# Query and key rows placed inside SBUF, one group of 32 rows and one PSUM bank per head, in a float32 attention and expert block

## The chip, the cores and the metric

One Trainium2 chip, 1 core. The metric is the device time of one execution in microseconds; the number compared is the median of the runs shown.

## The reference, cut to what matters

```python
x = x + xattn(layernorm(x), ctx)      # x (4, 256, 128), ctx (4, 64, 64), 16 heads of 8
x = x + ffn(layernorm(x))             # 32 experts, 8 per token, and a shared one
# xattn, h = layernorm(x), scale = 1/sqrt(8):
att  = where(causal, q @ k.T * scale, -inf)         # q, k, v from h, 256 x 256 per head
attc = qc @ kc.T * scale                            # qc from h, kc, vc from ctx, 256 x 64
out  = (softmax(att) @ v + softmax(attc) @ vc) @ Wp + bp
```

Everything is float32. The kernel keeps that precision by splitting a value into a rounded part (`hi`) and the rest (`lo`) and adding three products.

## The kernel before

The kernel is written engine by engine with semaphores; nothing schedules it but the order of its code. It has three parts.

*Prologue.* Tokens are normalized and transposed, and `project(b)` (PE) computes keys, queries and context queries of batch b as columns of tokens, with 128 rows (16 heads of 8). ScalarE rounds them (L699), VectorE takes the rest (L918). To get rows for the score products, SP writes keys and queries to three DRAM tensors, `key_dram`, `ckey_dram` and `query_dram` (L394, L412), and reads them back in another order (`read_keys` L425, `read_queries` L431, context keys L478). The weights' columns are permuted first, so that the writes can be made in one piece per head (`grouped`, `stacked`). What comes back is 96 rows: for each of 4 heads, 3 parts (hi, lo, hi for queries; hi, hi, lo for keys) of 8 rows. `key_blocks` holds keys block-diagonally, so that one product gives the scores of 4 heads side by side; the blocks between are constants that VectorE and ScalarE copy in (`blocks_const`, `ckey_const`), with 4 more rows of -1 that subtract each query's maximum.

*Attention.* 16 steps i, 4 batches b of 4 groups g of 4 heads. Per step, `natural(i)` (PE L1295, L1296, L1312) computes scores with queries on the partitions, in banks 0 to 3; `maxima(i)` (DVE L979, L983, L988) takes row maxima in three parts, each handed over alone; `turn_max(i)` (PE L1324) turns them to rows, `shift(i)` (ACT L714) copies 4 rows beside the queries; `scores(i, c)` (PE L1338, L1343, L1347), c = 0 to 3, computes the scores again with keys on the partitions and the maximum subtracted, each in one of two banks, 4 and 5; `exps` (ACT L725) takes one bank at a time; POOL zeroes above the diagonal (L616, L620); `attend_self` (L1360, L1365) and `attend_context` (L1372) multiply with the values, 4 heads writing to 4 different groups of 32 partitions; `copy_out` (ACT L732), `turn_out` (PE L1382) and `normalize` (DVE) finish. The order on PE is scores(i, 0 and 1), turn_max(i+1), natural(i+2), scores(i, 2), turn_out(i-2), scores(i, 3), attend(i-1). Probabilities of even steps lie in `probs_even`, of odd steps in the memory of `keys`, so that exps(1) waits until all keys are in DRAM (`wrote_k`). Batches alternate between two copies of the rows. Between the steps stand small pieces for finished batches (output projection, second norm, router).

*FFN.* 34 items, each an expert pair or the shared expert with a chunk of 512 tokens, and a last output copy.

The queue of SP is strictly in order: writes and reads of batch 0, context keys, writes of batches 1 to 3, reads of batch 1, small loads, FFN weights of 6 units, reads of batches 2 and 3, other weights. POOL writes the context keys (L394, called with `pool`), makes constants and normalizes the last four token tiles (L557).

Of the kernel before, what the change touches and what calls it, by code (L numbers as in the profile page):

```python
# [5 lines left out]
F32 = mybir.dt.float32  # L19
# [20 lines left out]
WRITES = ((0, 1), (1, 2), (2, 4))  # L40
NORM_GROUPS = ((0, 2), (2, 4), (4, 8))
SHIFT_ROW = PARTS * GROUP * D
ROWS = SHIFT_ROW + GROUP
PART = GROUP * D
EXPERTS, TOP, INNER = 32, 8, 64
# [33 lines left out]
B_NAT0, B_NATC, B_NAT1, B_ST, B_OUT, B_MISC = 0, 1, 2, 4, 6, 7  # L79
# [5 lines left out]
def build(nc, x, ctx, w, out):  # L85

    with ExitStack() as stack:
# [7 lines left out]
        key_dram = nc.dram_tensor("key_dram", (GROUP, PARTS * D, GROUPS, TOKENS), F32, kind="Internal").ap()  # L95
        ckey_dram = nc.dram_tensor("ckey_dram", (GROUP, PARTS * D, GROUPS, CTX_KEYS), F32, kind="Internal").ap()
        query_dram = nc.dram_tensor("query_dram", (GROUP, PARTS * D, GROUPS, 2, TOKENS), F32, kind="Internal").ap()
# [7 lines left out]
        key_const = sb("key_const", [P, GROUP, CTX])  # L105
        minus_half = sb("minus_half", [P, TILES])
        spread = sb("spread", [P, PAIRS, P], F32R)
# [6 lines left out]
        w_ctx = sb("w_ctx", [CTX_C, 3, C])  # L114
# [4 lines left out]
        qkc_bias = sb("qkc_bias", [4, 2, C])  # L119
# [21 lines left out]
        row_max = sb("row_max", [P, 2, 4, GROUP], F32R)  # L141
        probs_even = sb("probs_even", [P, 4, CHUNK])
# [19 lines left out]
        with ExitStack() as attention:  # L162
            queries = sb("queries", [P, 2, 2, TOKENS], F32R, until=attention)
            ckeys = sb("ckeys", [P, 2, CTX_KEYS], F32R, until=attention)
            query_rows = sb("query_rows", [P, 2, GROUPS, 2, SEQ], F32R, until=attention)
            key_blocks = sb("key_blocks", [P, 2, GROUPS, GROUP, SEQ], F32R, until=attention)
            ckey_blocks = sb("ckey_blocks", [P, GROUPS, BATCH, GROUP, CTX], F32R, until=attention)
            spread_f = sb("spread_f", [P, SPREAD_UNITS, P], until=attention)
            keys = sb("keys", [P, 2, TOKENS], F32R, until=attention)


        probs = [probs_even[:, :, :],
                 keys[:, :, :].rearrange("p h (c n) -> p (h c) n", n=CHUNK).bitcast(F32)]
# [25 lines left out]
        placed_q = [sem(f"placed_q{k}") for k in range(2)]  # L199
# [188 lines left out]
        def write_keys(sp, dram, parts, rounded, split, done):  # L388

            sp.wait_ge(*rounded)  # L390
            for part, half in enumerate(KEY_PARTS):
                if half:
                    sp.wait_ge(*split)
# [1161 lines left out]
```

## Time and profile before

| | us |
|---|---|
| median of 3 runs | 251.88 |
| lowest, highest | 250.64, 252.55 |
| span of the profiled execution | 250.6 |
| the fastest run, as long as that execution | 250.64 |
| busy PE, DVE, ACT, POOL | 197.4, 159.9, 133.4, 86.1 |

The profile is of one execution on one core. PE is TensorE, PEld its weight loads (they overlap PE), DVE VectorE, ACT ScalarE, POOL GpSimd, SP the queue that issues most transfers; a small q (SPq, POOLq) means the issuing of a transfer. A row of the timeline has the start, the time from the first to the last end of the merged instructions, the engine, the line, the operation, output and inputs, the count, and in brackets the idle time of the engine before it with what ended it. Ends of matmuls are modelled and overlap, so the pace of matmuls is read from their starts. The chain of waits is followed back from the last instruction.

### The profile page before, as it was taken

How to read it: one execution, taken by the hardware profiler on the slowest of the kernel's cores; microseconds unless marked ns; L12 is line 12 of the kernel's file. 1: busy time of each engine (PE TensorE's matmuls, PEld its weight loads, DVE VectorE, ACT ScalarE, POOL GpSimd, SP SyncE). 2: the span in 40 equal slices, each digit the busy share in tenths (PEclk: the TensorE clock that was granted, in tenths of full speed). 3: DMA queues.
4: the chain of work that ended last, by engine and by line, in shares of the span. 5: the costliest groups of instructions: out<-in, count | busy, mean ns of one | idle time of the engine just before them, and what ended most of it. 6: DMA issues, size and time to landing. Idle time of an engine off the chain costs nothing.

```text
span 250.6 us, 3757 instructions
## 1 busy us (share of the span) xinstructions
PE 197.4 (79%) x1211; PEld 147.5 (59%) x1221; DVE 159.9 (64%) x349; ACT 133.4 (53%) x242; POOL 86.1 (34%) x128
## 2 busy tenths in 40 slices
PE   0789009744404999999998998887999999999984
PEld 0578007523203776777765765565788888887762
DVE  6987005850002566677788565897758888879883
ACT  5334005514301576778677787837455666565561
POOL 7684000010004454345647554234443534221000
PEclk9999999995555799999999999998999999999999
DMA  4132383222375324025010211100000310000002
GB/s 123 45 98 84 125 175 104 99 102 102 125 233 142 98 86 105 3 63 128 0 35 9 56 34 35 28 0 0 4 0 21 82 39 3 1 1 0 0 3 84
DMA packets 26053, 15.51 MB, mean 62 GB/s; under 512 B 12463, under 2 KB 24786, under 8 KB 26034
## 3 DMA queue, kind: packets, MB, share of 16 engines
q1 hardware_dynamic: 25186, 14.77, 21.1%
q0 software_dynamic: 496, 0.40, 0.7%
q8 instruction: 10, 0.16, 0.3%
q10 hardware_dynamic: 352, 0.10, 0.2%
q14 instruction: 9, 0.07, 0.1%
HBM read 9.62 MB, written 5.64 MB: 61 GB/s over the span
## 4 chain that ended last, share of the span: by engine, by line
PE 58%; DMA 11%; SPq 11%; DVE 7%; ACT 4%; issue 4%; POOL 3%; DVEq 0%; POOLq 0%; ACTq 0%
PE psum L1212 10%; PE psum L1214 9%; PE psum L1213 9%; DMA query_rows<-query_dram 6%; SPq L412 5%; DMA query_dram<-queries 5%; PE psum L1296 5%; SPq L425 3%; PE psum L1372 3%; PE psum L1360 3%; PE psum L1496 3%; PE psum L1338 3%; PE psum L1382 3%; SPq L394 2%; PE psum L1343 2%
## 5 line engine op out<-in xcount | busy, mean ns | idle before, releaser
L979 DVE TENSOR_REDUCE row_max<-psum 128x4 fp32r<-128x512 f32 x16 | 11.0, 690 | 50.2 <-PE psum L1296 50.2
L815 ACT ACTIVATE gate<-psum,bias_cols 128x512 f32<-128x512 f32 (+2 forms) x35 | 23.5, 675 | 31.2 <-PE psum L1214 31.2
L1296 PE MATMUL psum<-key_blocks,query_rows 96*128 96x512 f32 x48 | 25.0, 564 | 12.1 <-DMA query_rows<-query_dram 12.1
L1155 DVE SCALAR_TENSOR_TENSOR gated<-psum,bias_cols,gate 128x512 f32<-128x512 f32 x32 | 24.0, 749 | 10.7 <-ACT gate L815 10.0
L592 POOL TENSOR_TENSOR w_ffn_lo<-w_ffn,w_ffn_hi 128x384 fp32r<-128x384 f32 x17 | 20.4, 1200 | 25.4 <-ACT w_ffn_hi L739 25.4
L1212 PE MATMUL psum<-xT_hi,w_ffn_hi 128*128 128x512 f32 x66 | 27.2, 412 | 0.0
L1214 PE MATMUL psum<-xT_hi,w_ffn_lo 128*128 128x512 f32 x66 | 26.2, 397 | 0.0
L1213 PE MATMUL psum<-xT_lo,w_ffn_hi 128*128 128x512 f32 x66 | 25.9, 393 | 0.0
L725 ACT ACTIVATE keys<-psum 128x512 f32<-128x512 f32 x32 | 18.7, 600 | 10.0 <-DMA key_dram<-keys 7.8
L1168 DVE TENSOR_TENSOR hid<-gated,psum 128x512 f32<-128x512 f32 x32 | 21.8, 682 | 1.3 <-PE psum L1496 0.6
L725 ACT ACTIVATE probs_even<-psum 128x512 f32<-128x512 f32 x32 | 18.9, 597 | 5.5 <-PE psum L1343 4.3
L822 ACT CAST hid_hi<-hid 128x512 fp32r<-128x512 f32 (+1 forms) x33 | 20.3, 616 | 2.3 <-DVE hid L1168 1.7
L1295 PEld LDWEIGHTS psum<-causal,ident_bf 128*128 128x128 bf16 x32 | 3.2, 100 | 29.0 <-issue 28.5
L983 DVE TENSOR_REDUCE row_max<-psum 128x4 fp32r<-128x1024 f32 x16 | 19.4, 1215 | 0.6 <-PE psum L1296 0.6
L1295 PE MATMUL psum<-causal,ident_bf 128*128 128x512 bf16 x22 | 9.3, 423 | 13.0 <-DMA query_rows<-query_dram 13.0
L862 DVE TENSOR_TENSOR hid_lo<-hid,hid_hi 128x512 fp32r<-128x512 f32 (+2 forms) x27 | 18.6, 693 | 1.1 <-ACT hid_hi L822 0.9
L616 POOL TENSOR_SCALAR_AFFINE_SELECT probs_even<-probs_even 128x512 f32<-128x512 f32 x8 | 5.1, 635 | 34.0 <-ACT probs_even L725 34.0
L732 ACT COPY o_sb<-psum 128x512 f32<-128x512 f32 x16 | 9.4, 588 | 13.3 <-PE psum L1372 13.3
L1212 PE MATMUL psum<-hid_hi,w_ffn_hi 128*128 128x512 f32 (+2 forms) x35 | 14.4, 410 | 1.1 <-DVE hid_lo L862 1.0
L1343 PE MATMUL psum<-query_rows,key_blocks 100*128 100x128 f32 x64 | 10.1, 283 | 6.3 <-ACT keys L725 6.3
L1343 PEld LDWEIGHTS psum<-query_rows,key_blocks 100*128 100x128 f32 x64 | 10.3, 209 | 7.8 <-ACT keys L725 6.7
L1212 PEld LDWEIGHTS psum<-xT_hi,w_ffn_hi 128*128 128x128 f32 x66 | 12.7, 192 | 3.5 <-issue 1.0
(184 smaller groups left out, 496.1 us busy)
## 6 DMA issues: line engine op xcount, KB each, us to landing
query_rows<-query_dram SPq DMA_DIRECT2D x4, 768.0 KB, 5.8
query_dram<-queries SPq DMA_DIRECT2D x6, 256.0 KB
key_blocks<-key_dram SPq DMA_DIRECT2D x16, 96.0 KB
query_dram<-queries SPq DMA_DIRECT2D x3, 512.0 KB
w_ffn<-in_L_ffn_Wg SPq DMA_DIRECT2D x16, 64.0 KB, 2.0
w_ffn<-in_L_ffn_Wu SPq DMA_DIRECT2D x16, 64.0 KB, 2.1
w_ffn<-in_L_ffn_Wd SPq DMA_DIRECT2D x16, 64.0 KB, 2.1
key_dram<-keys SPq DMA_DIRECT2D x6, 128.0 KB
```

What stands on the lines that cost most here:

```text
L592: ins = pool.tensor_tensor(w_ffn_lo[:, k, :, :], w_ffn[:, k, :, :], w_ffn_hi[:, k, :, :].bitcast(F32), ALU.subtract).then_inc(ffn_lo, 1)
L725: act.activation(probs[i % 2][:, c, :], bank(B_ST + c % 2), ACT.Exp, scale=SCALE).then_inc(exp_done, 1)
L815: act.activation(gate[rows_of(n), n % 3, part], psum[of, B_GATE + n % 2, part], ACT.Silu, bias=bias_cols[of, BIAS_GATE + u:BIAS_GATE + u + ...
L822: act.copy(hid_hi[rows_of(n - 1), (n - 1) % 3, :], hid[rows_of(n - 1), (n - 1) % 3, :]).then_inc(hid_rounded, 1)
L983: dve.tensor_reduce(to[:, 1, :], psum[:, B_NAT1:B_NAT1 + 2, :].rearrange("p k (j c) -> p j k c", j=GROUP), AX.XY, ALU.max).then_inc(max_do ...
L1155: dve.scalar_tensor_tensor(out=gated[:, n % 3, :], in0=bank(B_UP + n % 2), scalar=bias_cols[:, BIAS_UP + u:BIAS_UP + u + 1], in1=gate[:, n ...
L1168: dve.tensor_tensor(hid[:, n % 3, :], gated[:, n % 3, :], bank(B_WIDE + n % 2), ALU.mult).then_inc(hid_done, 1)
L1212: pe.matmul(dst, w_hi, x_hi, start=start, stop=False, skip_group_check=True)
L1213: pe.matmul(dst, w_hi, x_lo, start=False, stop=False, skip_group_check=True)
L1214: return pe.matmul(dst, w_lo, x_hi, start=False, stop=stop, skip_group_check=True)
L1296: return pe.matmul(to, query_rows[0:KR, b % 2, g, 0, P * q:P * (q + 1)], blocks[:, :, P * k:P * (k + 1)], start=not diagonal, stop=True, s ...
L1343: ins = pe.matmul(psum[:, to, P * j:P * (j + 1)], key_blocks[0:ROWS, b % 2, g, j, P:SEQ], query_rows[0:ROWS, b % 2, g, 0, P:SEQ], start=Tr ...
```

## The change

Keys and queries no longer go to DRAM. The permuted weights are gone; per batch b and group g, 3 transfers copy 32 rows of `keys` to every fourth partition of `key_rows` (offset by the part), and 3 copy 32 rows of `queries` (self and context, 512 columns) to `query_rows`. The context keys are placed likewise by POOL's queue. A head then has partitions 32j to 32j + 31: 8 rows of each of 3 parts and 8 free ones (slot 3), which hold -1 in the keys and 0 in the queries. `natural(i)` first lays the mask over 4 banks and then makes 16 products, each of one head's 32 rows into that head's bank. `turn_max` passes the 4 x 128 query columns through the identity into bank 7 and adds the maxima, which are stored so that they land on the head's slot 3; `shift` copies all 128 rows to a new tile `shifted`. The scores are two rounds p of two heads, one bank per head (self scores in columns 0 to 383, context in 384 to 511), and the context scores use `ckey_pairs`, keys of two heads made by VectorE from `ckey_rows` with a mask (`parity`). One exp covers two banks. Probabilities have two copies of their own. The late token tiles are normalized by VectorE.

```diff
-        key_dram = nc.dram_tensor("key_dram", (GROUP, PARTS * D, GROUPS, TOKENS), F32, kind="Internal").ap()
...
+        def place_keys(eng, b, g):
+            mine = slice(PART * g, PART * (g + 1))
             for part, half in enumerate(KEY_PARTS):
+                eng.dma_start(key_rows[part:P:SLOT, b % 2, g, :].bitcast(F32),
+                              keys[mine, half, tokens(b)].bitcast(F32)).then_inc(placed[b % 2][g], 16)
+        def place_queries(eng, b, g):
+            mine = slice(PART * g, PART * (g + 1))
+            for part, half in enumerate(QUERY_PARTS):
+                eng.dma_start(query_rows[part:P:SLOT, b % 2, g, :, :].bitcast(F32),
+                              queries[mine, half, b, :, :].bitcast(F32)).then_inc(placed[b % 2][g], 16)
+        def place_batch(sp, b):
+            if b < 2:
+                sp.wait_ge(rows_set[b], 2)
+            sp.wait_ge(qkc_rounded, 3 * b + 1)
+            sp.wait_ge(qkc_split, 3 * b + 1)
+            for g in range(GROUPS):
+                if b >= 2:
+                    sp.wait_ge(t_max, 4 * (b - 2) + g + 1)
+                    sp.wait_ge(m_st, 8 * (b - 2) + 2 * g + 2)
+                place_keys(sp, b, g)
+                if g == 0:
+                    sp.wait_ge(qkc_rounded, 3 * b + 3)
+                    sp.wait_ge(qkc_split, 3 * b + 3)
+                place_queries(sp, b, g)
@@ sync
-            write_token_keys(sp, 0)
-            write_queries(sp, 0)
-            read_keys(sp, 0)
-            read_queries(sp, 0)
...
+            place_batch(sp, 0)
+            place_batch(sp, 1)
@@ gpsimd
+            place_ctx_keys(pool, 0)
+            pool.memset(row_max[:, :, :, :].bitcast(F32), 0.0).then_inc(max_zeroed, 1)
+            pool.memset(query_rows[:, 1, :, :, :].bitcast(F32), 0.0).then_inc(rows_set[1], 1)
+            pool.memset(key_rows[:, 1, :, :].bitcast(F32), -1.0).then_inc(rows_set[1], 1)
+            for g in range(1, GROUPS):
+                place_ctx_keys(pool, g)
@@ scalar
+                for p in parts:
+                    act.wait_ge(m_st, 2 * i + p + 1)
+                    act.activation(probs[:, i % 2, 2 * p:2 * p + 2, :], psum[:, B_ST:B_ST + 2, :], ACT.Exp,
                                    scale=SCALE).then_inc(exp_done, 1)
@@ vector
+                dve.wait_ge(m_nat, i + 1)
+                dve.tensor_reduce(at(0), heads[:, :, 0:P], AX.X, ALU.max)
+                dve.tensor_reduce(to[:, 2:4, :].rearrange("p t (j r) -> p j t r", j=GROUP)[:, :, :, SHIFT],
+                                  heads[:, :, 3 * P:4 * P].rearrange("p j (t k) -> p j t k", t=2), AX.X, ALU.max)
+                dve.tensor_reduce(at(1), heads[:, :, P:3 * P], AX.X, ALU.max).then_inc(max_done, 1)
...
             maxima(0)
-            blocks_const(3, copy=1).then_inc(key_blocks1_set, 1)
+            dve.wait_ge(have_mask, 1)
+            for g in range(GROUPS):
+                dve.wait_ge(placed_ck[g], 48)
+            for h in range(2):
+                blocks, rows, mine = ckey_pair(h)
+                dve.tensor_scalar(blocks, rows, mine, None, ALU.mult).then_inc(ckey_pairs_set, 1)
             maxima(1)
@@ tensor, natural
+                for j in range(GROUP):
+                    pe.matmul(bank(B_NAT + j).rearrange("p (h k) -> p h k", h=2)[:, :, 0:P], ident_bf[:, :],
+                              causal[:, 0:2, :], start=True, stop=False, skip_group_check=True)
+                pe.wait_ge(placed[b % 2][g], 96 * (b // 2 + 1))
+                for s, t, cols in ((0, 0, slice(0, P)), (0, 1, slice(P, 3 * P)),
+                                   (1, 0, slice(3 * P, 3 * P + CTX)), (1, 1, slice(3 * P + CTX, 4 * P))):
+                    for j in range(GROUP):
+                        mine = slice(PART * j, PART * (j + 1))
+                        against = (ckey_rows[mine, g, CTX * b:CTX * (b + 1)] if s else
+                                   key_rows[mine, b % 2, g, 0:P * (t + 1)])
+                        ins = pe.matmul(psum[:, B_NAT + j, cols], query_rows[mine, b % 2, g, s, P * t:P * (t + 1)],
+                                        against, start=False, stop=True, skip_group_check=True)
@@ tensor, scores
+                for t, cols in ((0, slice(0, SEQ)), (1, slice(SEQ, SEQ + P))):
+                    for j in (2 * p, 2 * p + 1):
+                        mine = slice(PART * j, PART * (j + 1))
+                        pe.matmul(psum[:, B_ST + j % 2, cols], key_rows[mine, b % 2, g, P * t:P * (t + 1)],
+                                  shifted[mine, i % 2, 0, P * t:SEQ], start=True, stop=True, skip_group_check=True)
```

The order of the instructions on TensorE (PE) in one step of the attention, from the first scores of step 4 on, before; `query_rows` are queries, `key_blocks` and `ckey_blocks` the block-diagonal keys:

```order
L1338 MATMUL psum<-query_rows,key_blocks 128x256 x4
L1324 MATMUL psum<-ident_r,row_max 4x128 x4
L1295 MATMUL psum<-causal,ident_bf 128x512
L1296 MATMUL psum<-key_blocks,query_rows 128x512
L1312 MATMUL psum<-ckey_blocks,query_rows 128x256 x2
L1296 MATMUL psum<-key_blocks,query_rows 128x512
L1295 MATMUL psum<-causal,ident_bf 128x512
L1296 MATMUL psum<-key_blocks,query_rows 128x512
L1343 MATMUL psum<-query_rows,key_blocks 128x128 x4
L1382 MATMUL psum<-ident,o_sb 128x128 x4
L1347 MATMUL psum<-query_rows,ckey_blocks 128x256 x2
L1360 MATMUL psum<-probs_even,value 9x256 x4
```

After, the same place; L1183 is the mask, L1194 are the products of 32 rows, L1203 the identity pass:

```order
L1222 MATMUL psum<-shifted,key_rows 128x256 x2
L1222 MATMUL psum<-shifted,key_rows 128x128 x2
L1226 MATMUL psum<-shifted,ckey_pairs 128x128 x2
L1203 MATMUL psum<-query_rows,ident_r 128x512
L1206 MATMUL psum<-ident_r,row_max 128x128 x4
L1183 MATMUL psum<-causal,ident_bf 128x2x128 x4
L1194 MATMUL psum<-key_rows,query_rows 128x128 x4
L1194 MATMUL psum<-key_rows,query_rows 128x256 x4
L1194 MATMUL psum<-ckey_rows,query_rows 128x64 x8
L1259 MATMUL psum<-ident,o_sb 128x128 x4
L1222 MATMUL psum<-shifted,key_rows 128x256 x2
L1222 MATMUL psum<-shifted,key_rows 128x128 x2
```

Three products of 512 columns and two of 256 in `natural` have become 16 of 64 to 256 columns; the scores come in two rounds instead of four, the second one behind the turned outputs.

SP's queue from the prologue's last loads on, before:

```order
L469 DMA b_wide<-in_L_xattn_bcv 128x128
L394 DMA key_dram<-keys 4x32x256 x3
L412 DMA query_dram<-queries 4x64x256 x3
L425 DMA key_blocks<-key_dram 24x4x256 x4
L431 DMA query_rows<-query_dram 96x8x256
L478 DMA ckey_blocks<-ckey_dram 24x16x64 x4
```

And after, where the second pair of rows is repeated for three further groups of batch 0 and four of batch 1 before the next load:

```order
L429 DMA w_ctx<-in_L_xattn_Wcv 64x128
L431 DMA b_wide<-in_L_xattn_bv 128x128
L431 DMA b_wide<-in_L_xattn_bcv 128x128
L359 DMA key_rows<-keys 32x256 x3
L366 DMA query_rows<-queries 32x512 x3
```

Writes and reads through DRAM have become 6 small transfers per group.

## Rows read from the trace of the kernel before

**Rows 1.** Page, busy time, share of the span and instructions of each engine

```profile
PE 197.4 (79%) x1211; PEld 147.5 (59%) x1221; DVE 159.9 (64%) x349; ACT 133.4 (53%) x242; POOL 86.1 (34%) x128
```

**Rows 2.** Busy time by stretch: bounds, length, engines (x instructions), clock, transfer share, GB/s

```profile
25.40:37.40 12.00, 0.00 (x0) 0.04 (x2) 0.38 (x1) 0.00 (x0) 0.00 (x0) 1.00 0.62 152
...
53.00:59.00 6.00, 0.34 (x2) 0.00 (x0) 1.94 (x3) 0.00 (x0) 0.00 (x0) 0.83 0.26 102
...
64.00:78.60 14.60, 1.66 (x10) 1.27 (x8) 0.00 (x0) 2.35 (x4) 0.00 (x0) 0.50 0.54 177
...
85.30:152.90 67.60, 65.68 (x605) 47.14 (x612) 47.40 (x116) 50.09 (x96) 34.46 (x60) 1.00 0.21 53
152.90:250.60 97.70, 89.50 (x405) 68.25 (x404) 76.83 (x151) 57.21 (x99) 27.70 (x24) 0.98 0.07 17
```

**Rows 3.** Chain of waits in order of time, from 12 us on: start, us, what

```profile
18.66 12.68 DMA query_dram<-queries
...
69.21 9.29 DMA query_rows<-query_dram
```

**Rows 4.** Timeline, where odd steps and step 4 begin

```profile
59.00 0.60 ACT L725 ACTIVATE keys<-psum 128x512 f32<-128x512 f32 x1 [7.85 <-DMA key_dram<-keys]
...
78.64 0.59 PE L1295 MATMUL psum<-causal,ident_bf 128*128 128x512 bf16 x1 [12.98 <-DMA query_rows<-query_dram]
...
81.19 0.95 PE L1343 MATMUL psum<-query_rows,key_blocks 100*128 100x128 f32 x4
```

**Rows 5.** Timeline of PE, first scores and one full step

```profile
45.84 0.64 PE L1338 MATMUL psum<-query_rows,key_blocks 100*128 100x256 f32 x4
...
94.75 0.73 PE L1338 MATMUL psum<-query_rows,key_blocks 100*128 100x256 f32 x4
...
95.57 0.39 PE L1295 MATMUL psum<-causal,ident_bf 128*128 128x512 bf16 x1
...
96.96 0.56 PE L1343 MATMUL psum<-query_rows,key_blocks 100*128 100x128 f32 x4
97.36 0.62 PE L1382 MATMUL psum<-ident,o_sb 128*128 128x128 f32 x4
97.74 0.48 PE L1347 MATMUL psum<-query_rows,ckey_blocks 100*128 100x256 f32 x2
98.15 0.62 PE L1360 MATMUL psum<-probs_even,value 128*9 128x256 f32 x8
98.59 0.40 PE L1365 MATMUL psum<-probs_even,value 128*9 128x128 f32 x8
98.92 0.63 PE L1372 MATMUL psum<-probs_even,cvalue 128*41 128x256 f32 x4
99.48 0.73 PE L1338 MATMUL psum<-query_rows,key_blocks 100*128 100x256 f32 x4
```

**Rows 6.** Timeline of ACT and DVE in a step, of POOL in the prologue

```profile
97.62 1.24 ACT L725 ACTIVATE keys<-psum 128x512 f32<-128x512 f32 x2 [0.45 <-PE psum L1343]
...
93.79 1.21 DVE L983 TENSOR_REDUCE row_max<-psum 128x4 fp32r<-128x1024 f32 x1
...
5.68 1.07 POOL L544 MEMSET value<- 128x1152 f32 x1
...
11.34 2.16 POOL L394 DMA_DIRECT2D ckey_dram<-ckeys  x3
...
14.14 1.45 POOL L540 TENSOR_TENSOR rstd<-var_eps,minus_half 128x4 f32<-128x4 f32 x1 [0.65 <-DVE var_eps L858]
```

**Rows 7.** Transfers: SP's issues, and the list of landings (KB each, us)

```profile
60.71 8.46 SPq L425 DMA_DIRECT2D key_blocks<-key_dram  x4
...
77.79 0.47 SPq L446 DMA_DIRECT2D w_ffn<-in_L_ffn_Wu  x1
...
88.79 3.22 SPq L425 DMA_DIRECT2D key_blocks<-key_dram  x4
...
ckey_dram<-ckeys POOLq DMA_DIRECT2D x3, 128.0 KB, 5.3
```

More of the change, by code:

```diff
@@ L367, in projected @@
                 return keys[:, half, tokens(b)]
-            return queries[:, half, n - 1, tokens(b)]
+            return queries[:, half, b, n - 1, :]
         def lo_done(n):
@@ L397, in write_token_keys @@
-        def write_token_keys(sp, n):
-            first, end = WRITES[n]
-            cols = slice(first * SEQ, end * SEQ)
-            write_keys(sp, key_dram[:, :, :, cols], keys[:, :, cols], (qkc_rounded, 3 * end - 2),
-                       (qkc_split, 3 * end - 2), wrote_k[n])
-        def write_queries(sp, n):
-            first, end = WRITES[n]
-            cols = slice(first * SEQ, end * SEQ)
-            sp.wait_ge(qkc_rounded, 3 * end)
-            for part in (0, 2, 1):
-                half = QUERY_PARTS[part]
-                if half:
-                    sp.wait_ge(qkc_split, 3 * end)
-                sp.dma_start(query_dram[:, D * part:D * (part + 1), :, :, cols].rearrange("j d g s n -> j (d g) s n"),
-                             queries[:, half, :, cols].bitcast(F32)).then_inc(wrote_q[n], 16)
@@ L531, in _ @@
             chain(pool.memset(minus_half[:, :], -0.5))
-            for name, r0 in (("bq", BIAS_Q), ("bcq", BIAS_CQ)):
-                pool.dma_start(qkc_bias[r0 - BIAS_Q:r0 - BIAS_Q + 1, 0, :], row(w[name])).then_inc(in_q_bias, 16)
+            pool.memset(key_rows[:, 0, :, :].bitcast(F32), -1.0).then_inc(rows_set[0], 1)
+            pool.memset(causal[:, :, :], 0.0).then_inc(g_chain, 1)
+            chained[0] += 1
             def first_rstd(k):
@@ L702, in _ @@
                     round_x(1)
-                    for g in range(1, 2):
-                        ins = ckey_const(g)
-                    ins.then_inc(ckey_blocks_set, 1)
                 if b == 1:
@@ L764, in _ @@
                     shift(i + 1)
-                exps(i, (1,))
                 if i == 2:
@@ L800, in _ @@
             act.wait_ge(have_ffn_bias, 1)
-            for done in wrote_q:
-                act.wait_ge(done, 48)
-            act.wait_ge(wrote_ck, 48)
+            for k in range(2):
+                for g in range(GROUPS):
+                    act.wait_ge(placed[k][g], 192)
+            for g in range(GROUPS):
+                act.wait_ge(placed_ck[g], 48)
+            act.wait_ge(m_nat, STEPS)
             for n in range(ITEMS + 1):
@@ new lines, in natural, with turn_max @@
+                ins.then_inc(m_nat, 1)
+            def turn_max(i):
+                b, g = divmod(i, GROUPS)
+                pe.wait_ge(max_done, i + 1)
+                take_misc(shift_placed, i + 1)
+                pe.matmul(bank(B_MISC).rearrange("p (s n) -> p s n", s=2), ident_r[:, :], query_rows[:, b % 2, g, :, :],
+                          start=True, stop=False, skip_group_check=True)
+                for n in range(4):
+                    ins = pe.matmul(psum[:, B_MISC, P * n:P * (n + 1)], row_max[:, i % 2, n, :],
+                                    ident_r[:, :], start=False, stop=True, skip_group_check=True)
+                ins.then_inc(t_max, 1)
```

362 lines of the change are left out of this document (107 added, 255 removed).

## The prediction

> **What bounds the kernel now.** I read the page's busy lines first: TensorE is busy 79% of the span [rows 1], which is a mean over unlike stages. The table by stretches cuts the span into them [rows 2]. From 25.4 to 37.4 no compute engine works and the transfer engines are 0.62 busy; from 53.0 to 59.0 and from 64.0 to 78.6 it is the same picture with 0.34 and 1.66 us of TensorE work. From 85.3 to 152.9, 13 of the 16 steps of the attention run, TensorE busy 65.68 of 67.6 us; from 152.9 to the end the FFN takes 97.7 us. So there are three regimes: waits on transfers ahead of 85, a stage bound by TensorE, and an FFN that the change does not edit.
>
> Third view: the chain of waits names the transfers. `query_dram<-queries` holds it for 12.68 us from 18.66 on, and 9.29 us of it ahead of step 4 are `query_rows<-query_dram` [rows 3]. ScalarE stands 7.85 us before its first exp into `keys`, since odd steps put their probabilities where the keys lie and these must have left for DRAM first; TensorE stands 12.98 us before step 4 because batch 1's rows are not there [rows 4]. Steps 0 to 2 (scores at 45.84 to scores at 85.3) so take 39.5 us, where a later step takes 67.6 / 13 = 5.2 us [rows 2, 5].
>
> Why are these transfers slow? From 53 to 59 the writes of queries keep 0.26 of the sixteen engines busy at 102 GB/s, about four engines' worth [rows 2]. The Trainium skill has a rule that fits ("DMA: Bandwidth & Descriptors", on why a DMA increments its semaphore by 16): a transfer uses the largest count up to 16 that divides the outermost dimension of both its sides. The write's outer dimension is 4 heads, the new transfers' 32 rows, so by it four engines become sixteen; the trace agrees with the four. The sum below does not use it.
>
> **The change, part by part.** (a) DRAM is out of the path. Per batch and group of heads SP now issues 3 transfers of 32 rows by 1 KB and 3 of 32 rows by 2 KB, 24 per batch. Nothing before has this shape. The low end is an issue of 0.47 us (`w_ffn`, 64 KB); the high end is `key_blocks` (96 KB, through DRAM), 3.22 / 4 = 0.81 us each when the queue was empty and 8.46 / 4 = 2.1 us behind the big writes [rows 7]. I take 0.47, since these are smaller than the 64 KB row or equal to it and have no writes ahead of them. A batch then takes 24 x 0.47 = 11.3 us. Batch 0's keys are ready about when POOL could send the context keys, 11.34 [rows 6], so it is issued by 22 and batch 1 by 34, each group landing alone; even at 0.81 a group's six take 4.9 us, less than a step. Later batches wait for a freed slot and then for 2.8 us per group: hidden by the steps, and SP's weight loads stand where they stood. The wait for `wrote_k` ahead of odd steps goes with the shared buffer.
>
> (b) What is late next at the start. TensorE projects batches 0 to 2 until 25.4 and is then ready; there `natural(0)` starts instead of at 37.4. But the first scores also need `ckey_pairs`, and their rows come over POOL's queue. Before, POOL ends its third `rstd` at 14.14 + 1.45 = 15.6; a POOL transfer costs 2.16 / 3 = 0.72 us, a memset 1.07 us per 1152 elements [rows 6]. Now behind that `rstd` stand 3 transfers (2.2), memsets of 1024 + 2048 + 1024 elements (3.8) and 9 transfers (6.5): 28.1 us. The landing takes some 2 us (a landing of 128 KB from this queue took 5.3 [rows 7]), and VectorE then makes two passes over 1024 columns, each at most the 1.21 of its reduction over as many [rows 6]. That gives 31 to 36; I take 33. VectorE stands in that wait with `maxima(1)` behind it, so step 0 also pays the maxima: 2.5 us of reductions less 1 that overlaps, +1.5. Scores at 33 and not 45.8 is 12.8 us. Steps 0 to 2 then cost 3 x 5.45 + 1.5 = 17.9 instead of 39.5: 21.6 us.
>
> (c) TensorE per step. Before, the rows add up to 99.48 - 94.75 = 4.73 us [rows 5]: the first scores and the turned maxima 0.82 (95.57 - 94.75), `natural` 1.39, the other scores 0.40 and 0.41 with the turned outputs, 0.38, between them, attention outputs 0.44 + 0.33 + 0.56. No engine waits inside it. Now `natural` has 4 mask passes of 256 columns (as many columns as before, 0.46), and 16 pieces of 32 rows, in four rounds of four heads, each head in its own rows of the array and its own bank. Do four such pieces run side by side? The nearest row is L1360: eight matmuls of 256 columns (two passes for each of four heads) in 0.44 us, where the pace of `natural` (1.39 us for 6 x 512 columns, 0.23 per 512) would make 0.93; the heads write different partitions and overlap [rows 5]. That is the same trick on the columns of the array; on its rows the trace shows nothing. Bounds: 0.10 us per round if they overlap (a 128-column piece of L1343, its weight load included, is 0.40 / 4), 0.10 us per piece if not. I take 0.12 per round: 0.46 + 0.48 + 0.12 = 1.06 us. The last 0.12 is a change of tiling: L1365 streams half of L1360's columns but takes 0.33, not 0.22, and L1372 0.56 against 0.44 for the same columns [rows 5]. The turned maxima get the identity pass of 512 columns (0.23) and weights of 128 columns instead of 4 (4 x 0.11): 0.67. The scores become twice (two rounds of tiles, two context pieces: 4 x 0.12; two changes of tiling, 0.24) = 1.44. Turned outputs 0.48, attention outputs 1.33 as before. That is 2.11 us of scores and turned maxima where 1.63 were. Sum 4.98 us, +0.25 per step, over 13 steps 3.2 us given back.
>
> A rule speaks against this part: the Trainium skill ("TensorEngine Tiling (Array Packing)", Key Properties) says that a change of tiling mode drains TensorE. The trace agrees that something is paid, 0.11 to 0.12 us beside L1365 and L1372, but the same page gives independent tiles their own loads and matmuls at once, which only the column tiles show here. By the first alone, at nine changes a step against three, the step would be near 5.3 us.
>
> (d) ScalarE and VectorE. Two exps of 512 columns take 1.24 us [rows 6]; one over two banks lies between that and 1.0, so two of them with shift and copy (one bank each, half of that row) are 3.3 to 3.7 us per step, below 4.98. The scores' two banks have no second copy: scores, exp, scores, exp in turn is 2 x (0.7 + 1.25) = 3.9 us, covered as well. VectorE reduces the same columns; 1.21 us is the largest of its three [rows 6], and they now start only when all of `natural` is done: 1.06 + 2.5 + 0.3 = 3.9 us before the banks are free, again less than a step. I cost these at nothing; if TensorE's step fell under 4 us they would set it. The copies that filled constants leave the prologue and bring nothing behind (b).
>
> Sum: -12.8 - 21.6 + 3.2 = -31.2 us. The span was 250.6, so 219.4. The profiled execution is as long as the fastest run shown (250.64), 1.3 us below the median 251.88, so I add this: **220.7 us**, 12% faster.
>
> **The rivals.** *Pieces one by one (15%).* Weight loads of the row tiles do not overlap, 0.11 us a piece: `natural` +1.28, scores +0.36, together +1.6 us a step, 26 us over 16 steps: 247. For it: L1343's pieces are paced by their loads (0.10 each for 128 columns, which at 0.23 per 512 would stream in 0.06) [rows 5]. Against it: L1360's eight overlap. The Trainium skill ("TensorE: Matmul & The Clock Gate", LDWEIGHTS) has a load cost the same for 32 rows as for 128; by that alone small pieces save nothing, which is this rival.
>
> *The start only changes its wait (7%).* POOL's chain of (b) or batch 1's transfers at 0.8 us hold the first scores to 45: 12 us lost, 233. For it: the 5.3 us landing; against it: natural(4) needs only batch 1's first group.
>
> *Slower: the clock (6%).* In the trace the granted clock is 1.00 after steady work and falls to 0.50 in the idle stretches [rows 2]. At 0.50 (1.2 GHz) `natural` takes 81.19 - 78.64 = 2.55 us instead of 1.39 [rows 4, 5]: 1.83 times. Pieces of 32 rows use a quarter of the array; if they don't keep the level up, the new step is 4.98 x 1.83 = 9.1 us, 4.1 more, 62 us over 15 steps: 282. It turns the sign where the loss passes 31 us, with more than half of the steps at 0.50.
>
> *Slower: transfers pace the steps (3%).* At 2.1 us each, 96 transfers end at 212 and the FFN only then: 10 + 202 + 12 + 97.7 = 322. The break-even is near 1.4 us per transfer, above what an empty queue shows.
>
> **How the numbers follow.** Forecast 69%, its own range 207 to 232: low with rounds at 0.10 without changes of tiling (8 x 0.02 + 0.46, so -0.6 us a step, 10 us) and scores at 29, if context keys are ready earlier than 15.6 and both passes are short (-4), high with 0.5 us more per step (8) and scores at 36 (3). Beside it 15, 7, 6 and 3%. To leave out no more than 2 in 10, the range goes to 247 and takes in pieces one by one. About 1% is what a measurement of this kernel tells from no change. Faster by over 1%: 69 + 7 + 15, 91%. The clock case is split: a partial loss that eats the gain, within 1%, 3%; the other 3 and the transfers' 3 are slower, 6%.
>
> **What would show it.** Right: `natural(0)` at 22 to 26 us, first scores at 31 to 35, no idle TensorE stretch over 3 us afterwards; starts of four L1194 pieces within 0.02 us of each other, 1.0 to 1.1 us for `natural`; the gap from step to step 5.2 to 5.6 us; FFN 97 to 98 us. Wrong: pieces 0.1 us apart, SP's small transfers at 0.8 us or more apiece, a granted clock of 0.5 in the steps, or VectorE or ScalarE named as the releaser of `natural` and scores in most steps.

## The result, and the profile after

The changed kernel took 285.58 us (median of 4 runs, 282.99 to 288.92), the kernel before 252.22 us in the same session (250.64 to 252.86): a ratio of 1.128, 95% interval 1.120 to 1.136. It is slower by 13%, where 220.7 us and 12% faster were forecast. The profiled execution is the shortest of the four, with a span of 281.2 us.

First the page of the kernel after: busy time by engine, and the TensorE clock in 40 slices of 7 us.

```profile
PE 255.7 (91%) x1477; PEld 180.3 (64%) x1477; DVE 159.7 (57%) x348; ACT 125.4 (45%) x204; POOL 87.9 (31%) x134
...
PEclk9999855555555555555555695579999999999999
```

Beside [rows 1] only TensorE changed much: 58 us more busy time. VectorE has as much as before, ScalarE less. The clock row says why: from the sixth slice to the 26th it stands, but for the 23rd and 24th, at five tenths. The stretches (bounds, length, then busy time of PE, PEld, DVE, ACT, POOL with the number of instructions, granted clock, transfer share, GB/s):

```profile
25.10:32.50 7.40, 5.25 (x61) 4.28 (x62) 5.74 (x11) 1.79 (x4) 0.53 (x2) 1.00 0.31 79
32.90:59.80 26.90, 24.04 (x161) 16.55 (x159) 10.68 (x18) 9.59 (x14) 6.57 (x13) 0.50 0.36 87
59.80:159.10 99.30, 98.78 (x633) 64.64 (x632) 36.56 (x85) 36.59 (x51) 27.68 (x49) 0.50 0.11 28
159.10:169.40 10.30, 8.69 (x87) 6.40 (x86) 5.17 (x16) 6.84 (x12) 3.31 (x6) 1.00 0.16 40
169.40:184.00 14.60, 13.96 (x83) 7.61 (x83) 4.75 (x19) 6.00 (x9) 5.08 (x8) 0.50 0.06 15
184.00:281.20 97.20, 87.93 (x396) 66.75 (x388) 75.40 (x146) 55.91 (x97) 26.32 (x23) 0.99 0.07 17
```

The stretches without TensorE work of [rows 2] are gone, as forecast. The last stretch, the FFN, takes 97.2 us, as forecast. Between them, from 59.8 us on, TensorE works almost without a gap and at half its clock: 98.78 of 99.30 us busy at 0.50 (1.2 GHz). Before, 13 steps ran with 65.68 of 67.60 us busy at 1.00 [rows 2]. The busy share is about the same in both, so it is not what separates the two levels.

The waits of the first steps don't separate them either. The kernel before had the longer ones, was also at 0.50 in this part, and rose after a short piece of full work; from 85.3 us on it stands at 1.00 [rows 2]. Its stretch ahead of that:

```profile
78.60:84.20 5.60, 5.56 (x28) 4.15 (x32) 2.41 (x5) 2.01 (x5) 4.59 (x10) 0.50 0.62 139
```

The Trainium skill ("TensorE: Matmul & The Clock Gate", Part 1) says that the throttled state is the default and that activity releases it, by how busy TensorE has been. These rows qualify it: an engine that a profile calls 99% busy can stay throttled for 99 us.

The same operations at both levels, from the timeline of TensorE in the kernel after (start, duration of the group, engine, line, tiles, rows by columns of the weights, operand, count):

```profile
62.11 0.80 PE L1194 MATMUL psum<-key_rows,query_rows 32*128 32x128 f32 x8
...
63.11 1.11 PE L1259 MATMUL psum<-ident,o_sb 128*128 128x128 f32 x4
...
160.95 0.61 PE L1183 MATMUL psum<-causal,ident_bf 128*128 128x256 bf16 x4
161.49 0.50 PE L1194 MATMUL psum<-key_rows,query_rows 32*128 32x128 f32 x8
...
162.07 0.66 PE L1259 MATMUL psum<-ident,o_sb 128*128 128x128 f32 x4
```

Sixteen pieces of `natural` with their masks take 162.07 - 160.95 = 1.12 us at 1.00. From the next rows, of one step at 0.50, masks and pieces take 63.11 - 61.11 = 2.00, and the step from one `turn_max` to the next 69.02 - 59.76 = 9.26 us:

```profile
59.76 0.79 PE L1203 MATMUL psum<-query_rows,ident_r 128*128 128x512 f32 x1
...
61.11 1.08 PE L1183 MATMUL psum<-causal,ident_bf 128*128 128x256 bf16 x4
...
69.02 0.79 PE L1203 MATMUL psum<-query_rows,ident_r 128*128 128x512 f32 x1
```

The start went as forecast. TensorE begins `natural(0)` at 25.11 and the first scores at 32.52 us (45.84 before [rows 5]):

```profile
25.11 1.06 PE L1183 MATMUL psum<-causal,ident_bf 128*128 128x256 bf16 x4
26.10 0.50 PE L1194 MATMUL psum<-key_rows,query_rows 32*128 32x128 f32 x8
...
30.78 0.50 PE L1203 MATMUL psum<-query_rows,ident_r 128*128 128x512 f32 x1 [2.15 <-DVE value L820]
...
32.52 0.43 PE L1222 MATMUL psum<-shifted,key_rows 32*128 32x256 f32 x4
```

The masks at 25.11 take 1.06 us, the pace of 0.50 (1.08 at 61.11), though the clock of the stretch reads 1.00; the pieces at 26.10 have the fast pace. So the clock row is not to be trusted everywhere: of the other executions of this kernel one reads 0.993 on average and is 3.0 us longer (284.2 us) than the profiled one, which reads 0.745. Where the two differ, the level is read here from the pace of the matmuls. SP's transfers cost 0.6 us each (three in 1.87 us) and land in 2.1 us or less; no engine waits for one after the start.

The issue of three is a row of SP's timeline; the landing, a row of the page's list of issues:

```profile
23.62 1.87 SPq L366 DMA_DIRECT2D query_rows<-queries  x3
```

```profile
query_rows<-queries SPq DMA_DIRECT2D x48, 64.0 KB, 2.1
```

### The profile page after: what moved, and what is told of

It is laid out like the page before. It is cut to its first block, busy times and chain, and to the rows that moved or that the text cites. A ratio compares the mean times of both kernels' runs of the same rounds, so it can differ in the third digit from the quotient of the medians.

```text
span 281.2 us, 4302 instructions
## 1 busy us (share of the span) xinstructions
PE 255.7 (91%) x1477; PEld 180.3 (64%) x1477; DVE 159.7 (57%) x348; ACT 125.4 (45%) x204; POOL 87.9 (31%) x134
## 4 chain that ended last, share of the span: by engine, by line
PE 76%; DVE 9%; issue 6%; POOL 4%; ACT 4%; DVEq 0%; POOLq 0%; ACTq 0%
PE psum L1110 9%; PE psum L1112 8%; PE psum L1111 8%; PE psum L1226 6%; PE psum L1222 6%; PE psum L1249 5%; PE psum L1194 5%; PE psum L1240 5%; PE psum L1183 5%; PE psum L1259 4%; PE psum L1206 4%; PE psum L1203 4%; DVE x L796 3%; POOL hid_lo L587 2%; PE psum L1243 2%
## 5 line engine op out<-in xcount | busy, mean ns | idle before, releaser
L651 ACT ACTIVATE probs<-psum 128x1024 f32<-128x1024 f32 x32 | 32.8, 1024 | 59.5 <-PE psum L1226 59.5
L565 POOL TENSOR_SCALAR_AFFINE_SELECT probs<-probs 128x512 f32<-128x512 f32 x32 | 20.4, 636 | 100.9 <-ACT probs L651 100.9
L1222 PEld LDWEIGHTS psum<-shifted,key_rows 32*128 32x128 f32 x128 | 15.1, 288 | 11.3 <-issue 10.5
L1222 PE MATMUL psum<-shifted,key_rows 32*128 32x128 f32 (+1 forms) x128 | 20.7, 417 | 1.3 <-ACT probs L651 1.2
L1226 PE MATMUL psum<-shifted,ckey_pairs 64*128 64x128 f32 x64 | 21.2, 428 | 0.0
L1226 PEld LDWEIGHTS psum<-shifted,ckey_pairs 64*128 64x128 f32 x64 | 15.3, 295 | 3.6
L1249 PE MATMUL psum<-probs,cvalue 128*41 128x256 f32 x64 | 16.9, 625 | 0.0
L1206 PEld LDWEIGHTS psum<-ident_r,row_max 128*128 128x128 f32 x64 | 16.0, 306 | 1.4
L1259 PE MATMUL psum<-ident,o_sb 128*128 128x128 f32 x64 | 15.9, 395 | 1.0 <-ACT shifted L643 0.9
L1183 PE MATMUL psum<-causal,ident_bf 128*128 128x256 bf16 x64 | 16.3, 406 | 0.0
```

What stands on the lines that cost most here:

```text
L651: act.activation(probs[:, i % 2, 2 * p:2 * p + 2, :], psum[:, B_ST:B_ST + 2, :], ACT.Exp, scale=SCALE).then_inc(exp_done, 1)
L1183: pe.matmul(bank(B_NAT + j).rearrange("p (h k) -> p h k", h=2)[:, :, 0:P], ident_bf[:, :], causal[:, 0:2, :], start=True, stop=False, skip ...
L1206: ins = pe.matmul(psum[:, B_MISC, P * n:P * (n + 1)], row_max[:, i % 2, n, :], ident_r[:, :], start=False, stop=True, skip_group_check=True)
L1222: pe.matmul(psum[:, B_ST + j % 2, cols], key_rows[mine, b % 2, g, P * t:P * (t + 1)], shifted[mine, i % 2, 0, P * t:SEQ], start=True, stop ...
L1226: ins = pe.matmul(psum[:, B_ST + t, 3 * P:4 * P], ckey_pairs[pair, g, b, :, :].rearrange("p h k -> p (h k)"), shifted[pair, i % 2, 1, P * ...
L1249: ins = pe.matmul(psum[64 * j:64 * j + 32 + D + 1, B_OUT, SEQ:2 * SEQ], cvalue[:, b, 2 * g + j, :], probs[:, i % 2, 2 * j:2 * j + 2, 3 * P ...
```

## The experiments

Thirteen more kernels ran. Theory A: TensorE stays at its low level because most products of the new step use 32 or 64 rows of the array. Theory B: the waits of the first steps, or the changes of tiling, bring it down. Theory C: columns per time count, not rows. The tool of most runs is a product that computes nothing that is used: 512 columns, over 128 rows ("dense"), at a place where its bank is free. At 1.00 four of them take 0.99 us.

### e1_dense4: four dense products per step

```diff
                 # natural(i), ahead of the mask passes
+                for j in range(4):
+                    pe.matmul(bank(B_NAT + (j % GROUP), 4 * C), w_qkv_hi[0:128, 1, :],
+                              w_qkv_hi[0:128, 0:4, :], start=True, stop=True, skip_group_check=True)
```

> The changed kernel with four more products of 128 rows by 512 columns per step, ahead of the mask passes of natural, into banks that the mask then overwrites: work that serves nothing. Theory A (the 32-row and 64-row pieces count too little for the clock, the stage is dense but thin): the granted clock of the steps is 1.00 again, a filler costs 0.23 us, a step 5.3 + 0.9 + 0.5 for the tails = 6.7 us, total 32.5 + 16 x 6.7 + 97 = 237 us plus about 1. Theory B (the level is lost in the waits of steps 0 and 1 and does not come back while tilings change, whatever the rows): the clock stays 0.50, a filler costs 0.43 us, 1.7 us a step, total about 310 us.

Measured: 264.49 us (259.82 to 268.19), 21 us faster than the change although it does 16 us more work. Its stretches:

```profile
33.70:50.80 17.10, 14.45 (x80) 10.69 (x79) 4.84 (x6) 4.24 (x5) 2.73 (x5) 0.50 0.33 79
50.80:102.00 51.20, 48.27 (x511) 32.62 (x510) 26.42 (x51) 24.89 (x35) 18.14 (x35) 1.00 0.26 63
102.00:108.80 6.80, 6.80 (x38) 4.85 (x37) 0.42 (x1) 2.50 (x4) 0.83 (x2) 0.50 0.01 2
108.80:129.30 20.50, 18.45 (x186) 12.47 (x182) 13.73 (x38) 10.28 (x16) 6.86 (x13) 1.00 0.04 11
...
149.80:166.90 17.10, 16.12 (x97) 9.00 (x97) 5.31 (x20) 7.22 (x11) 5.52 (x9) 0.50 0.08 20
```

The level came back for most of the steps, with relapses; 264 us lies between the sizes expected by A (237) and B (310). In its long stretch at 1.00 a step can be read at the high level:

```profile
67.54 0.50 PE L1206 MATMUL psum<-query_rows,ident_r 128*128 128x512 f32 x1
...
68.28 1.15 PE L1183 MATMUL psum<-w_qkv_hi 128*128 128x512 f32 x4
69.27 0.61 PE L1186 MATMUL psum<-causal,ident_bf 128*128 128x256 bf16 x4
...
70.38 0.66 PE L1262 MATMUL psum<-ident,o_sb 128*128 128x128 f32 x4
70.97 0.44 PE L1225 MATMUL psum<-shifted,key_rows 32*128 32x256 f32 x4
...
71.70 0.62 PE L1243 MATMUL psum<-probs,value 128*9 128x256 f32 x8
...
73.04 0.44 PE L1225 MATMUL psum<-shifted,key_rows 32*128 32x256 f32 x4
...
73.78 0.50 PE L1206 MATMUL psum<-query_rows,ident_r 128*128 128x512 f32 x1
```

73.78 - 67.54 = 6.24 us, less 0.99 for the products: 5.25 us, where 4.98 were forecast.

### e2_thin4: the same four products over 32 rows

The same edit with `w_qkv_hi[0:32, ...]` on both sides (and all four into the first of the banks).

> The same four fillers with 32 rows instead of 128: as many columns and instructions, a quarter of the array. Theory A: the clock stays 0.50, the fillers cost 0.43 us each, total about 310 us. Theory B and a theory C (columns streamed count, not rows) give the same result as for 128 rows, whichever that is.

Measured: 321.14 us (one run). One stretch says it: without a break at 0.50, busy 186.52 of 191.10 us.

```profile
32.30:223.40 191.10, 186.52 (x1052) 118.67 (x1053) 58.31 (x139) 60.43 (x87) 42.73 (x75) 0.50 0.12 30
```

The same columns at the same places as in e1, only on a quarter of the rows, give nothing back: C falls, and place and waits are those of e1 (there is one more change of tiling a step), so the waits of B don't explain the difference either. Nor do B's changes of tiling bring the level down by themselves: e1 has those of the changed kernel and runs at 1.00 for 51 us.

### e4_before32: the kernel before, with its score products over 32 rows

```diff
-                KR = SHIFT_ROW
+                KR = 32
```

and `0:32` in place of `0:ROWS` in the score products of the kernel before; nothing is subtracted ahead of the exps and most of each sum is left out. Its order, columns, waits and tilings by column stay; tiles of 32 rows, and with them changes of tiling by rows, are new.

> The kernel before with 32 of its 96 or 100 rows in all score products (only one head's share is computed and nothing is subtracted; same instructions, columns, banks and transfers, one tiling of 32 rows added). Theory A: the clock falls to 0.50 in the steps that ran at 1.00, a step goes from 5.2 to 9 us, total about 300 us; if only the share of thin work decides, it may hold part of the time, 260 to 300. Theory B: no change, 250 to 256 us, since no wait is added.

Measured: 318.6 us (one run) against 252 with full rows. Groups by form, first of this whole run, then of the kernel before in its steps from 85.3 us on (count, busy us, mean ns):

```profile
L1295 PE MATMUL psum<-causal,ident_bf 128*128 128x512 bf16 x32 | 19.5, 609 | 24.4 <-DMA query_rows<-query_dram 24.4
```

```profile
L1295 PE MATMUL psum<-causal,ident_bf 128*128 128x512 bf16 x14 | 5.5, 390 | 0.0
```

The mask pass is the same instruction in both and takes 609 instead of 390 ns. The stretches of this run:

```profile
85.00:150.00 65.00, 65.00 (x303) 36.91 (x299) 22.16 (x45) 23.46 (x41) 15.74 (x30) 1.00 0.15 39
...
153.40:221.60 68.20, 68.20 (x334) 39.69 (x331) 26.44 (x78) 29.47 (x55) 21.18 (x34) 0.50 0.07 17
```

In the second of them the clock reads 0.50. In the first it reads 1.00, but the mask passes there have the low pace (0.61 and 0.65 us each), so the level is read from them. Products over fewer rows, in the old kernel and without a new wait, bring its steps to the low pace. They come with changes of tiling that this run doesn't separate from the rows; e1 beside e2 does that.

### e3_nat128: `natural` over all rows in the changed kernel

```diff
-                        against = (ckey_rows[mine, g, CTX * b:CTX * (b + 1)] if s else
-                                   key_rows[mine, b % 2, g, 0:P * (t + 1)])
-                        ins = pe.matmul(psum[:, B_NAT + j, cols], query_rows[mine, b % 2, g, s, P * t:P * (t + 1)],
+                        against = (ckey_rows[:, g, CTX * b:CTX * (b + 1)] if s else
+                                   key_rows[:, b % 2, g, 0:P * (t + 1)])
+                        ins = pe.matmul(psum[:, B_NAT + j, cols], query_rows[:, b % 2, g, s, P * t:P * (t + 1)],
```

Each piece then sums over four heads, so that the maxima, which serve as a shift alone, are others.

> The 16 pieces of natural read all 128 rows instead of one head's 32 (the sum over four heads takes the place of each head's scores; same instructions, columns and banks). Theory A: the clock of the steps is 1.00, the pieces no longer overlap and cost 0.11 us each, natural 2.2 to 2.3 us, step 6.4 to 6.9 with tails, total 232 to 242 us. Theory B: clock 0.50, natural 4.1 us, total about 305 us.

Measured: 293.07 us (one run). The clock was 1.00 in 34.10 us and 13.60 us of the steps and 0.50 in the rest; not the 232 to 242 us that A was made to predict.

```profile
34.70:85.90 51.20, 48.71 (x251) 38.91 (x251) 13.70 (x23) 14.42 (x20) 9.61 (x19) 0.50 0.27 64
85.90:120.00 34.10, 31.42 (x300) 23.90 (x299) 17.30 (x35) 15.44 (x21) 11.60 (x21) 1.00 0.14 36
```

More rows in one part of the step, with one stretch of row tiles fewer, bring the level back in part of the time. Inside that stretch the run also gives the price of the pieces one after another, at the high level:

```profile
90.94 0.61 PE L1183 MATMUL psum<-causal,ident_bf 128*128 128x256 bf16 x4
91.31 1.16 PE L1194 MATMUL psum<-key_rows,query_rows 128*128 128x128 f32 x8
...
93.12 0.65 PE L1259 MATMUL psum<-ident,o_sb 128*128 128x128 f32 x4
```

The 16 pieces take 93.12 - 91.31 = 1.81 us over all rows, and 162.07 - 161.49 = 0.58 us as row tiles of the changed kernel: 3.1 times less. From the first mask pass to the first piece it is 0.37 us here and 161.49 - 160.95 = 0.54 there, where a change of tiling stands between; four passes by their own pace, 0.11 each, are 0.44. An estimate from these rows puts that change at 0.10 to 0.17 us. The scores, the other products over few rows, were left as they are; that they are what keeps it down for the rest was not tried.

### e5_half: dense products in the first steps only

```diff
+                for j in range(4 if i < 9 else 0):
```

> The changed kernel with the four dense products (128 rows, 512 columns, into the four banks of the natural scores ahead of the masks) in the steps 0 to 8 only; the steps 9 to 15 are those of the changed kernel. Theory A (TensorE falls to its low level because most of a step's products use 32 or 64 rows): the granted clock is 1.00 for most of the steps up to 8, as with four in every step, and reads 0.50 in nearly all of the steps after; seven steps then take 9.3 us instead of about 6.2 each, or 264 - 7 x 1.0 (products gone) + some 15 to 20 = 272 to 278 us. Theory D (the dense products only helped TensorE out of its fall at the start, and the level then holds itself): the clock stays at 1.00 and the time is below 264, at about 257.

Measured: 268.76 us (one run). The timeline at the end of the treated part (columns as before):

```profile
86.11 0.61 PE L1186 MATMUL psum<-causal,ident_bf 128*128 128x256 bf16 x4
...
92.66 0.61 PE L1186 MATMUL psum<-causal,ident_bf 128*128 128x256 bf16 x4
...
97.88 0.44 PE L1290 MATMUL psum<-ident,x_norm 128*128 128x128 f32 x2 [1.38 <-DVE o_norm L914]
...
100.09 1.08 PE L1186 MATMUL psum<-causal,ident_bf 128*128 128x256 bf16 x4
```

```profile
33.00:98.00 65.00, 58.97 (x588) 40.73 (x588) 32.30 (x59) 29.76 (x41) 20.91 (x40) 0.95 0.29 70
98.00:175.00 77.00, 74.80 (x457) 47.97 (x457) 28.99 (x85) 32.14 (x49) 22.22 (x37) 0.53 0.07 16
```

The last dense products start at 78.70. The masks at 86.11 and 92.66 belong to the first two steps without them and still have the fast pace; in the third the masks take 1.08 in place of 0.61 us, and the level stays low to the end of the stage. So the level does not hold itself once the products are gone, and D falls; but it held for some 20 us, and went after a wait of 1.38 us. The time lies beside A's range (272 to 278), a little under it.

### More products, and other places

> The changed kernel with the same four dense products per step as in the run at 264 us, but in three places: two ahead of the masks, one ahead of each of the two groups of scores. Theory A1 (the level falls where too few dense products come one after another for a while, so that an even spread holds it better): fewer stretches at 0.50 after the first 1.00, 245 to 260 us. Theory A2 (only the share of dense work in a whole step matters): the same pattern of lapses as before, 260 to 268 us.

> Six dense products per step: four ahead of the masks, one ahead of each group of scores. At the high level a step takes 4.98 + 6 x 0.25 = 6.5 us. Theory A: more dense work removes the lapses; 16 x 1.5 = 24 us over the forecast of 220.7, 245 us, and up to 253 with a start at the low level as in the run at 264. If the lapses stay as with four, it is some 268.

> Four dense products ahead of the masks in every step, and 24 of them in the step 0, where TensorE waits from 25.6 to 31.5 us for the first rows to be placed. Theory A with a level that remembers what TensorE has just done: it reads 1.00 from the start on, the 17 us at 0.50 from 33.7 are saved for the most part (17 us at low pace are some 9 at high pace): 264 - 8 = 256 us, less if the later lapses go too (237). Theory A2 (only the share within the steps matters): the fall at 33 comes anyway and the time stays at 264.

The edits: e6 has 2 in place of 4 ahead of the masks and one in `scores` behind its waits, into the bank of the scores; e7 has 4 ahead of the masks and the same in `scores`; e8 has `4 if i else 24` ahead of the masks. Measured: e6 261.12 us (253.48 to 273.99), e7 273.59 (272.17 to 275.13), e8 264.74 (261.43 to 272.74); the kernel before 252.13. In its shortest run, the profiled one, e6 held the level best of all profiled runs:

```profile
33.30:49.50 16.20, 14.42 (x76) 9.99 (x75) 4.84 (x6) 4.25 (x5) 2.74 (x5) 0.50 0.31 72
49.50:141.50 92.00, 87.14 (x871) 57.68 (x870) 48.98 (x112) 46.90 (x70) 34.74 (x62) 1.00 0.19 45
141.50:148.30 6.80, 6.49 (x36) 3.66 (x38) 0.82 (x3) 2.57 (x5) 2.29 (x4) 0.52 0.07 18
```

This run closes the account. Its span of 251.7 us is 32.3 over the forecast of 219.4. Of these, 64 products of 0.25 us are 16; 16.2 + 6.8 us at 0.50, where a step takes 9.26 for 5.25 us, are 23.0 x (1 - 5.25 / 9.26) = 10; a step 0.27 us longer than forecast is 4. The remaining 2 are left open. So with the level held, what the change removes is there.

The placement is not settled: e6's runs scatter over 20 us; its median lies in A2's range, its shortest run in A1's. Their mean granted clocks are 0.951, 0.914, 0.895 and 0.868 in the order of their times, so it is the time at the low level that differs. e7 missed both of its sizes and gives the simple form "more dense work, fewer relapses" no support: after 38 us its profiled run stands at 0.50 for 44 us in five stretches, that of e1, with four products, for 48 us in five. The 9 us between their medians are about what 32 more products of 0.25 us cost. In e8 TensorE is at 1.00 from 28.2 to 38.3 us, waits for 2.15 us in it, and falls anyway.

> The changed kernel with two dense products ahead of the masks, one ahead of each group of scores (the even spread that ran at 253.5 to 274 us, median 261.1) and now two ahead of the wait of each of the tails that stand between the steps (turned y, projection and so on, some 20 of them), where TensorE waits for the VectorE: in the run with six products a step the clock fell at 110 us right after 3.4 us in which TensorE waited 1.1 us for o_norm. Theory A3 (a fall needs few dense products together with a wait): the falls after the first 1.00 go, all runs lie near the fastest so far, 250 to 256 us. If the waits don't matter: 255 to 275 us as before, and some 5 us more for the products.

> As the run e9 with 24 dense products in place of two in the first step, where TensorE waits for the first rows to be placed (25.6 to 31.5 us). Theory A3: the level holds through the start as well, which saves up to half of the 17 us at 0.50: 242 to 250 us, faster than the kernel before. If the fall after 33 us has another cause (the waits of the steps 0 and 1): 250 to 256 us, as e9.

> As e10 with one product ahead of the masks in place of two, three per step. At the high level a step costs 0.25 us less, 4 us in all. If three hold the level: 238 to 246 us. If the dense share is then too small (theory A, and none would give 285 us): stretches at 0.50 come back, 255 to 275 us.

The edit of all three: two dense products at the head of each tail that stands between the steps, ahead of its wait (`for j in range(fill)` in `tail`). Measured: e9 263.90 us (262.09 to 277.31), e10 272.91 (268.08 to 280.07), e11 272.53 (266.12 to 282.76), before 252.48. None came near what A3 expects; e9 and e11 lie in the other range of their expectations, e10 above both of its ranges. e11's stretches show the odd shape of it:

```profile
38.00:79.70 41.70, 39.92 (x230) 25.88 (x228) 12.76 (x22) 11.78 (x17) 7.23 (x14) 0.51 0.27 64
79.70:174.10 94.40, 88.33 (x846) 58.95 (x846) 46.43 (x119) 48.43 (x71) 35.63 (x61) 1.00 0.12 28
```

With three products per step the level is 0.50 for 41.7 us, and then 1.00 without a relapse for 94.

> The changed kernel with dense products where TensorE waits at the start (24 in step 0, 10 in step 1, 8 ahead of the wait for the first shift), four ahead of the masks in the steps 2 to 4, two in the later ones, and one ahead of each group of scores; none in the tails. The run with 24 in step 0 alone held 1.00 until 35 us and then fell while TensorE waited 2.1 of 3.4 us. Theory A3 (the fall at the start comes from waits together with few dense products): 1.00 without a break from 25 to about 140 us and a time of 220.7 + 16 x 1.0 + 2 = about 239 us, under 246 in most runs. If waits of the start bring it down in spite of the products: 0.50 for 15 to 25 us near 38 us, and 250 to 262 us.

> As e12 with one product ahead of the masks in the steps 5 to 15, three per step in all. Three per step held 1.00 from 79 to 195 us in the profiled run of e11. If the start holds: 4 us less than e12, about 236. If it does not, the level comes back late, as in e11 (at 79 us), and the time is 255 to 270 us.

The edit: `(24, 10)[i] if i < 2 else (4 if i < 5 else 2)` ahead of the masks (e13: 1 at its end), 8 ahead of the wait for the first shift, one in each `scores`. Measured: e12 271.06 us (261.32 to 273.30), e13 278.62 (269.04 to 289.37), before 252.09. e12's stretches:

```profile
42.30:51.80 9.50, 8.29 (x72) 6.04 (x72) 4.84 (x6) 2.53 (x3) 1.31 (x3) 1.00 0.37 85
52.20:66.00 13.80, 13.80 (x71) 9.01 (x72) 2.42 (x3) 4.52 (x6) 3.09 (x6) 0.50 0.35 84
66.50:154.40 87.90, 82.95 (x816) 54.87 (x814) 46.53 (x109) 43.65 (x67) 32.71 (x58) 0.99 0.12 30
```

The level holds for 88 us, and both ends of the stage fall all the same; the case "waits of the start bring it down in spite of the products" is what the expectation describes, with 271 us even above its 250 to 262. e13 lies above both of its sizes. (The run with 24 products in the first step that the expectation of e12 speaks of kept 1.00 until 38.3 us, in e8, and not 35.) As a rule for where it falls, A3 failed five times, and no version of the changed kernel beat the one before: the nearest, one run of e6, took 253.48 us.

## Why the prediction was wrong

**Right.** The start: `natural(0)` at 25.11 (22 to 26 forecast), first scores at 32.52 (33). But steps 0 to 2, to the scores at 58.53, took 26.0 us where 17.9 were forecast: they already ran at 0.50. Step (a): issues 0.62 us (0.47 to 0.81), hidden. The row tiles run side by side: `natural` takes 1.12 us at the high level where 1.06 was forecast; one by one its pieces make it 2.18 (e3; 2.3 in the rival). Four pieces of one round start within 0.011 us, as the sign asked (0.02). Step (c) at that level is 5.25 us (e1) where 4.98 was forecast: turned outputs 0.59 for 0.48, turned maxima 0.74 for 0.67, masks and pieces 1.11 for 1.06, scores 1.47 for 1.44, attention outputs 1.34 for 1.33. The largest of these gaps is that of the turned outputs: 0.38 in [rows 5], 0.48 in the sum without a reason, 0.59 here, where a change of tiling follows them. Step (d): an exp over two banks takes 1.02 us and hides; TensorE waits once for an exp, 1.2 us. FFN 97.2 us for 97.7.

The row tiles' overlap was the one mechanism of (c) that no row of before showed, and it came in near the low end of its bounds. The Trainium skill ("TensorEngine Tiling (Array Packing)", Overview) offers row tiling as up to four times the speed for a contraction of 32. At one level of the clock the traces come near it, with 3.1 times; over the stage they don't, since the level was lost.

**Wrong: the level at which step (c) runs.** The sum took 4.98 us from rows at 1.00 and left the fall to 0.50 to a rival at 6%. That rival is what happened, in size too: 9.26 us a step (9.1 worked out), 285.6 us in all (282). The reason given for its low chance, that "the granted clock is 1.00 after steady work and falls to 0.50 in the idle stretches" [rows 2], was read from a kernel whose steps use 96 to 128 rows, so it could not tell "busy" from "busy over many rows". Those rows also have 1.00 in a stretch without any TensorE work (25.40 to 37.40), so they don't tie the level to steady work as the sentence has it. The runs do tell: e1 and e2 differ in the rows of four products (and in one change of tiling and the bank they write), and the level differs; e4 lowers the rows in the old kernel, and e5 takes the dense work away, and the level falls.

Of the profiled execution's time, 126.2 us (32.9 to 159.1) and 17.1 us (169.4 to 186.5) stand at 0.50. At 9.26 for 5.25 us that is 143.3 x 0.433 = 62 us, and 281.2 - 62 = 219.2, beside the forecast span of 219.4. The agreement is in part luck: a step 0.27 us longer than forecast is made good by smaller terms of the start, and not all of the 143 us is bound by TensorE.

**The bar for the sign** ("more than half of the steps at 0.50") was passed here, and the sign turned. No run tests where it lies: e1, with about a third of its stage low, lost too, but it has 16 us of added work.

What stays open: why the level falls where it does once dense products are there. Their number, their spread, and the waits of TensorE were each tried and none predicts it. Several falls come after a wait of TensorE (2.15 us in e8, 1.38 in e5), but one of 1.12 us at 100.77 in e6 brings none. The changed kernel itself rises to 1.00 at 159.1 us for 10 us, in steps like the others; the runs don't say why. That the low start is what makes the late steps stay low was not tried by itself; the kernel before had a low part ahead of 84.2 us and rose.

## What to carry to other kernels

Before products are cut into row tiles, compare the rows that the stage's products use with what they used before. A stage that is bound by TensorE can be 99% busy and lose its high clock. Here that made a step 1.76 times as long, more than the overlap and the earlier start give back. In an ablation, keep a dense product of known length in the loop as a gauge (the mask pass: 0.61 or 1.08 us), and price a rival about the clock by what the old kernel's rows could have shown, not by how steady its clock was. Padding with dense work gets the level back only in part and costs its own time.

## What the runs showed of the hardware that was not expected

- TensorE at 0.50 for 99 us while busy for 98.78 of them, and for 191 us in e2: continuous matmuls over 32, 64 and some over 128 rows did not raise the level in these stretches.
- Four dense products of 512 columns per step (0.99 us of 6.24) go with 1.00 for 51 us in e1; without them it is gone by the third step (e5).
- Six products per step (273.59 us) cost more time than four (264.49 and 261.12) and won back no more of the level: 44 us at 0.50 against 48 in e1.
- Sixteen pieces in row tiles of 32 rows take 0.58 us from the first start to the next instruction, weight loads included, and 1.81 us over all 128 rows one after another (e3): row tiles overlap. The change of tiling ahead of them costs 0.10 to 0.17 us, by an estimate from the same rows.
- One kernel's runs differ by far more once its level is unstable: 253.48 to 273.99 us for e6, 269.04 to 289.37 for e13, while the kernel before stays within 250.51 and 254.07 in all sessions.
